# A scan kernel with an FFN in its shadow: FFN steps placed later in the phase, the normalisation's bias made on POOL, z statistics and x loads moved

## The reference

```
# layer 1, for each batch entry; channels = 512, states = 16
u     = silu(causal_conv4(in_proj(ctx)))                 # [512 channels, 512 steps]
dt_lo, Bm, Cm = x_proj(u)
delta = softplus(dt_proj(dt_lo) + bias)
state[t] = state[t-1] * exp(delta[t] * A) + delta[t]*u[t]*Bm[t]      # 16 states a channel
y     = (sum_n state_n * Cm_n + D*u) * silu(layernorm(x))
x     = x + tanh(g_xattn) * y
# layer 2
h     = layernorm(x)
sc    = h @ Wr                       # 32 experts
g     = softmax(sc) kept on the two highest, normalised (+1e-8)
out   = sum_s g_s * (h @ U_s) @ V_s;   gate = g @ sigmoid(attr @ Wa)
x     = x + tanh(g_ffn) * out * (0.9 + 0.2 * gate)
```

## Time and profile before

| what | value |
|---|---|
| median of 3 runs | 624.99 us (624.39 to 625.16) |
| the profiled execution | 624.96 us, its span 623.2 us |
| PE matmul busy | 538.7 us, 86% |
| DVE busy | 467.7 us, 75% |
| POOL busy | 437.2 us, 70% |
| ACT busy | 362.0 us, 58% |
| mean granted PE clock | 0.956 of full speed |

### The profile page before, as it was taken

The page is one execution under the profiler, slowest core; times in us unless marked ns, Lnnn a source line. Parts: engine busy times, 40 slices in busy tenths (PEclk is TensorE's granted clock), DMA queues, the critical chain, the costliest instruction groups (busy, mean ns, idle before and its releaser), DMA issues.

```text
span 623.2 us, 9369 instructions
## 1 busy us (share of the span) xinstructions
PE 538.7 (86%) x3410; PEld 415.3 (67%) x3410; DVE 467.7 (75%) x775; ACT 362.0 (58%) x574; POOL 437.2 (70%) x253
## 2 busy tenths in 40 slices
PE   6643979798868899999989999999988989986987
PEld 2142869777767687768777777677776868674443
DVE  3517989878848999788889999778779797944330
ACT  3343786857735667575756767566666676432311
POOL 0056999979996878669988788589978787741000
PEclk9765999999987899999999999999999999998899
DMA  3196000115220001035120000153000000000001
GB/s 83 54 359 232 2 0 2 35 51 192 101 69 1 1 1 52 1 116 210 35 85 2 18 1 19 62 197 102 17 2 18 1 19 1 17 18 1 18 17 50
DMA packets 17408, 35.19 MB, mean 56 GB/s; under 512 B 5441, under 2 KB 5953, under 8 KB 17362
## 3 DMA queue, kind: packets, MB, share of 16 engines
q1 hardware_dynamic: 17362, 34.60, 16.1%
HBM read 30.13 MB, written 4.46 MB: 56 GB/s over the span
## 4 chain that ended last, share of the span: by engine, by line
PE 38%; POOL 24%; DVE 15%; issue 10%; ACT 8%; DMA 3%; SPq 1%; DVEq 0%; POOLq 0%; ACTq 0%
POOL state L437 14%; PE p_s L575 10%; DVE state L1029 9%; PE p_y L593 7%; POOL dbu L428 6%; PE p_f L622 3%; ACT da L799 3%; PE p_tr L548 3%; PE p_v L631 3%; PE p_pr L521 3%; DMA xs<-in_x 2%; PE p_s L631 2%; POOL du L417 2%; POOL diag_b L407 1%; PE p_s L514 1%
## 5 line engine op out<-in xcount | busy, mean ns | idle before, releaser
L437 POOL TENSOR_TENSOR state<-state,c_bc 128x1024 f32<-128x1024 f32 x128 | 302.1, 2366 | 87.7 <-DVE state L1029 87.5
L1029 DVE TENSOR_TENSOR_SCAN state<-da,p_s 128x512 f32<-128x512 f32 x192 | 230.4, 1210 | 24.7 <-PE p_s L575 23.4
L575 PEld LDWEIGHTS p_s<-diag_b,du_t 128*128 128x128 f32 x1536 | 196.6, 198 | 26.7 <-issue 22.1
L575 PE MATMUL p_s<-diag_b,du_t 128*128 128x128 f32 x1536 | 209.8, 282 | 0.7 <-ACT du_t L775 0.7
L799 ACT ACTIVATE da<-delta,a_neg 128x512 f32<-128x512 f32 x192 | 136.2, 716 | 104.9 <-DVE state L1029 104.8
L593 PE MATMUL p_y<-ident,state 128*128 128x128 f32 x1024 | 144.2, 274 | 0.0
L593 PEld LDWEIGHTS p_y<-ident,state 128*128 128x128 f32 x1024 | 119.1, 142 | 10.1 <-issue 8.6
L1029 DVE TENSOR_TENSOR_SCAN state<-p_s,dbu 128x512 f32<-128x512 f32 x64 | 77.1, 1210 | 2.1 <-POOL dbu L428 2.1
L428 POOL TENSOR_TENSOR dbu<-du,b_bc 128x1024 f32<-128x1024 f32 x32 | 75.6, 2361 | 0.1
L799 ACT ACTIVATE p_s<-delta,a_neg 128x512 f32<-128x512 f32 x64 | 43.7, 688 | 28.9 <-DVE state L1029 28.7
L622 PE MATMUL p_f<-u_sb,h_t 128*128 128x512 f32 x96 | 47.7, 603 | 5.0 <-DVE gw L1118 5.0
(11 more groups left out here) (189 smaller groups left out, 621.6 us busy)
## 6 DMA issues: line engine op xcount, KB each, us to landing
c_bc<-bc_rows SPq DMA_DIRECT2D x32, 512.0 KB, 5.0
b_bc<-bc_rows SPq DMA_DIRECT2D x8, 512.0 KB, 4.5
xs<-in_x SPq DMA_DIRECT2D x16, 256.0 KB, 8.3
out<-ot SPq DMA_DIRECT2D x12, 256.0 KB, 2.0
cx<-in_ctx_t SPq DMA_DIRECT2D x4, 512.0 KB, 3.6
u_sb<-in_u_w SPq DMA_DIRECT2D x1, 1024.0 KB, 11.5
v_sb<-in_v_w SPq DMA_DIRECT2D x1, 1024.0 KB, 13.4
out<-state SPq DMA_DIRECT2D x4, 256.0 KB, 2.0
```

Of the source, the lines that this page charges most:

```text
L437: eng.tensor_tensor(pair, pair, c_bc[:, 2 * p:2 * p + 2, :], ALU.mult).then_inc(po_cs, 1)
L575: mm = eng.matmul(p_s[g % BANKS][:, t * P:(t + 1) * P], du_t[:, f % 2, t, :], diag_b[:, i, t, :], start=(t == 0), stop=(t == Q - 1))
L1029: eng.tensor_tensor_scan(slot(g), decayed, added, 0.0, ALU.mult, ALU.add).then_inc(ve_scan, 1)
```

## The change

Five edits.

1. Inside a phase, tile mid = f - 5: normed moves from the end of phase f - 1 (n = 15) to n = 1 of phase f, turn_h to n = 2, copy_h to n = 4, scores from n = 2 to n = 4, best_two to n = 4 and 5, exp_scores to n = 7, the gates from n = 4, 5, 6 to n = 6, 7, 8, with combine(f + 1) and gate_y(f - 1, 0) between their parts. times_u_weights moves from n = 8, 10, 12 to n = 10, 11, 12. turn_gated moves from n = 2 of the next phase to n = 15 of the same, copy_gated to n = 1 of the next. TURN and the head of the drain follow.
2. The bias of the normalisation is made by POOL, behind the power, and no longer by DVE (f_statistics part 3, L1067).
3. f_statistics parts 1 and 2 wait for POOL's work of four tiles earlier.
4. x of batch entry 0 is loaded ahead of C rows 5 to 7.
5. In phase 0 the z statistics move from n = 0 to 3 to n = 8 to 11, and scale_of_z(0) on POOL from after times_b(0, 5) to after times_c(0, 5).

```diff
@@ POOL
                 eng.tensor_tensor(fr[:, i, 0:1], fmv[:, i, 1:2], minus_half[:, 0:1], ALU.pow).then_inc(po_fs, 1)
+                eng.wait_ge(po_fs, 2 * T + 1)
+                eng.tensor_scalar(fr[:, i, 1:2], fmv[:, i, 0:1], fr[:, i, 0:1], -1.0, ALU.mult, ALU.mult).then_inc(po_fs, 1)
...
-                if k == 0:
+                if k == 0 and b:
                     scale_of_z(b)
...
+                if f == 0:
+                    scale_of_z(0)
                 times_c(f, 6)
@@ SP
-            for p in range(2, PAIRS):
+            for p in range(2, 5):
                 broadcast_c(0, p)
             for k in range(Q):
                 load_x(0, k)
+            for p in range(5, PAIRS):
+                broadcast_c(0, p)
@@ PE
                         if mid >= 0:
+                            turn_h(mid)
+                    if n == 4:
+                        if mid >= 0:
                             scores(mid)
-                        if tail >= 0:
-                            turn_gated(tail)
-                    if n == 4:
...
-                    if n == 8 and mid >= 0:
-                        times_u_weights(mid, [0, 1])
                     if n == 9 and f + 5 < F:
                         in_projection(f + 5)
                     if n == 10 and mid >= 0:
+                        times_u_weights(mid, [0, 1])
+                    if n == 11 and mid >= 0:
                         times_u_weights(mid, [2])
...
-                    if n == 15 and f >= Q:
-                        turn_h(f - Q)
+                    if n == 15 and mid >= 0:
+                        turn_gated(mid)
@@ DVE
-                    if f == 0 and n < Q:
-                        z_statistics(n)
+                    if f == 0 and 8 <= n < 8 + Q:
+                        z_statistics(n - 8)
...
-                    if n == 2 and mid >= 0:
+                    if n == 4 and mid >= 0:
                         best_two(mid, 0)
                         best_two(mid, 1)
-                    if n == 3 and mid >= 0:
+                    if n == 5 and mid >= 0:
                         best_two(mid, 2)
-                    if n == 4 and mid >= 0:
+                    if n == 6 and mid >= 0:
                         gates(mid, 0)
...
+                    if n == 7:
+                        if mid >= 0:
+                            gates(mid, 1)
+                        if f < LAST:
+                            combine(f + 1)
+                        if mid >= 0:
+                            gates(mid, 2)
+                    if n == 8:
+                        if mid >= 0:
+                            gates(mid, 3)
+                        if f:
+                            gate_y(f - 1, 0)
+                        if mid >= 0:
+                            gates(mid, 4)
+                            gates(mid, 5)
```

More of the change, by code:

```diff
@@ L77, in flamingo @@
             pass_through("sz", f - 1)
-        if f >= 6:
-            pass_through("hug", f - 6)
+        if f >= 5:
+            pass_through("h", f - 5)
         if f % Q == Q - 1 and f < LAST:
@@ L83, in flamingo @@
             pass_through("du", f + 1)
-        if f >= Q:
-            pass_through("h", f - Q)
-    for kind, i in [("sz", 15), ("hug", 10), ("h", 12), ("h", 13), ("hug", 11), ("h", 14), ("h", 15),
+        if f >= 5:
+            pass_through("hug", f - 5)
+    for kind, i in [("sz", 15), ("h", 11), ("h", 12), ("h", 13), ("hug", 11), ("h", 14), ("h", 15),
                     ("hug", 12), ("hug", 13), ("hug", 14), ("hug", 15)]:
@@ L227, in flamingo @@
         ve_fs = sem("dve_residual_statistics")
-        ve_nmr = sem("dve_residual_bias")
         ve_top = sem("dve_top")
@@ L703, in _ @@
             add_y(LAST, 9)
+            turn_h(11)
+            add_y(LAST, 10)
+            add_y(LAST, 11)
             scores(11)
-            add_y(LAST, 10)
-            turn_gated(10)
-            add_y(LAST, 11)
             add_y(LAST, 12)
@@ L826, in normed @@
             def normed(T):
-                eng.wait_ge(ve_nmr, T + 1)
+                eng.wait_ge(po_fs, 2 * T + 2)
                 if T and T < F - Q:
@@ L903, in _ @@
                         eng.activation(aw[:, :], y_rows[:, 0:S], ACT.Exp, scale=-1.0).then_inc(ac_k, 1)
-                    if n == 1 and mid >= 0:
-                        copy_h(mid)
+                    if n == 1:
+                        if mid >= 0:
+                            normed(mid)
+                        if tail >= 0:
+                            copy_gated(tail)
                     if n == 3:
@@ L910, in _ @@
                             place_residual(tail)
[L911 to L918, removed]
-                        softplus(f + 1, 0)
+                    if n == 4 and mid >= 0:
+                        copy_h(mid)
+                    if n == 5 and turning:
+                        copy_small(b + 1)
+                    if n == 7:
+                        if f < LAST:
+                            softplus(f + 1, 0)
+                        if mid >= 0:
+                            exp_scores(mid)
                     if n == 8:
@@ L939, in _ @@
                             copy_du(f + 1)
-                        if f >= Q:
-                            normed(f - Q)
                         if f + 5 < F:
                             tanh_v(f + 5)
+            normed(11)
+            copy_gated(10)
+            copy_sz(LAST)
             copy_h(11)
-            copy_sz(LAST)
             place_residual(10)
-            copy_gated(10)
             place_residual(11)
@@ L1058, in f_statistics @@
                     eng.wait_ge(ve_fs, FOPS * T + 1)
+                    if T >= Q:
+                        eng.wait_ge(po_fs, 2 * (T - Q) + 2)
                     eng.bn_aggr(fmv[:, i, :], fst[:, i, :]).then_inc(ve_fs, 1)
-                elif part == 2:
+                else:
                     eng.wait_ge(ve_fs, FOPS * T + 2)
+                    if T >= Q:
+                        eng.wait_ge(po_fs, 2 * (T - Q) + 2)
                     eng.tensor_scalar(fmv[:, i, 1:2], fmv[:, i, 1:2], EPS, None, ALU.add).then_inc(ve_fs, 1)
-                else:
-                    eng.wait_ge(po_fs, T + 1)
-                    if T >= Q:
-                        eng.wait_ge(ac_h, T - Q + 1)
-                    eng.tensor_scalar(fr[:, i, 1:2], fmv[:, i, 0:1], fr[:, i, 0:1], -1.0, ALU.mult, ALU.mult).then_inc(ve_nmr, 1)
             def best_two(T, part):
@@ L1226, in _ @@
                     gate_hu(11)
-            for T in range(F - Q, F):
-                f_statistics(T, 3)
             for T in (12, 13):
```

18 lines of the change are left out of this document (5 added, 13 removed).

## The result

| | before | after |
|---|---|---|
| median | 625.08 us (624.39 to 625.45, 4 runs) | 630.21 us (629.26 to 634.95, 4 runs) |
| profiled execution, span | 623.2 us | 628.1 us (629.87 in all) |
| PE matmul busy | 538.7 us | 539.5 us |
| DVE busy | 467.7 us | 457.3 us |
| POOL busy | 437.2 us | 440.6 us |

The account below looks back on a forecast made before the run. PE and DVE were taken as two bounds side by side. Terms: -6.0 - 5.6 + 3.4 + 1.8 + 3.4 + 7.6 + 0.5 + 4.0 + 1.9 - 8.8 = +2.2, so 627.2 us; 8 in 10: 613 to 637.

Parts of the forecast that it names:

- The cycle of a plain phase: Plain phases from 6 on: late gates make PE wait before times_u_weights, 8.7 + 24.5 = 33.2 us against 31.5, +1.7.
- Rival 4: Phases stay at 31.5 us because PE's idle time before times_u_weights does not appear: 609 us, chance 0.09.
- L1104's wait to the end of POOL's instruction: Gates after combine: L1104, issued 1.1 us into POOL's instruction, waits to its end; bounds 0.15 to 2.36 us.
- the early entry: Phase 5: L1104 gets in one POOL instruction earlier, giving -7.5 us instead of -5.2.
- main case: Phase 5: L1104 meets a POOL working without a gap until 213 and waits to about 202.6.
- Phases 4 and 5: DVE's 7.3 us wait at L1067 goes, with one fall of PE's clock counted: -5.6 us.
- Rival 2: L1104 gets in late in POOL's instruction, or another POOL order makes it cheap: 617 us, chance 0.10.
- The removed wait buys nothing here: Phases from 6 on: L1067's wait is gone, but DVE stands 2.9 us ahead of scan 6 waiting for make_dbu(6).
- PE's clock: Gaps before times_u_weights bring 1.2 GHz: +1.8 us in phases 6 to 10, +7.6 in 11 to 14, +1.9 in 15.
- rivals 1 and 3: 1: clock holds wholly or half, 614 or 620.5 us, 0.24; 3: falls in every phase 5 to 15, 638, 0.15.
- Head: Phase 0: z statistics no longer wait for x, first scan of phase 1 earlier: -6 us, bounds 0 and -8.
- Tail: Drain: normed(12) no longer waits for four tiles' statistics, times_u_weights(12) starts at 573.9 instead of 582.67: -8.8 us.

Follow-up runs that it names:

- the scalar form: Changed kernel with the first instruction of gates part 2 as tensor_scalar, its second number a scalar of each partition: 614.82 us, ratio 0.9849.
- edit 4 alone: Kernel before with only x of batch entry 0 loaded ahead of C rows 5 to 7, z statistics unmoved: 621.13 us, ratio 0.9941.

## Why the prediction was right, and where it was not

*The cycle of a plain phase.* Right: 33.2 us forecast, 33.16 measured; turning phases 37.6 and 37.23; f = 8 33.2 and 33.71; f = 9 32.2 and 32.03. L1110 about 1.3 us (1.29), 1.84 behind a turning phase, 0.15 beside scale_of_z; the idle time ahead of times_u_weights 2 and 4 us (1.70 and 4.07); cheap, the cycle is 32.0 (32.08). The two pieces, 8.7 and 24.5 us, came as 8.5 and 24.7. Rival 4 is out by the same numbers.

*L1104's wait to the end of POOL's instruction.* Right, also for a late start, which no row of before had shown. The trace agrees with the Trainium skill's rule (SBUF — State Buffer, SBUF: two separate sides), that whichever starts first holds the shared ports to its end. In phase 5 it came at 198.79, 0.26 us before POOL's instruction ended (199.05), and took 0.28. That isn't the early entry which the forecast had named as worth 2.3 us: counted from the combine in phase 4, it ended 33.9 us on, where the forecast's main case had it (202.6 less 168.67). Phases 4 and 5 came to -7.0 and not -5.6 because the fall of the clock that was counted in phase 5 didn't come: the gap there was 0.68 us, and from times_u_weights to scan 6 of phase 6 it was 25.0 us, 26.5 forecast. Rival 2 is out.

*"The removed wait buys nothing here".* Wrong as a statement of worth, though the sum did not need it. I compared the wait with DVE's idle time ahead of scan 6, one place, and not with the scans, ACT's decays and copies and the shared bank behind it. The new cycle was worked out directly for a DVE without the wait, so its number held. But edit 2 (with 3), which I priced at nothing outside phase 4 and the drain, is the best of the five, and the order, priced at 1.7 us a plain phase, costs 2.4 against a kernel that has edit 2 (30.76 to 33.16). In all it takes away those 13 us and some 8 more.

*PE's clock.* Right in place: no fall in phases 6 to 10 (1.8 forecast), one in each from 11 to 15, so rivals 1 and 3 are out. Off in size: 1.4 to 1.7 us for a fall instead of 1.9. From the combine in 14 on, two falls and an L1110 of 2.25 us stand in the +10.7, where 8.3 was forecast (0.5, 4.0 and two falls). I haven't taken that stretch apart. With the scalar form, which had a fall in phase 14 and none in 15, it (499.11 to 558.20) was 3.9 us longer than before.

*Head.* Wrong by 4.4 us, the largest miss of a term. Some 2.4 of it were there at the first scan of phase 1, half of that since the slow clock in phase 0 came that the -6 mostly left out. Then 2.0 more were lost: I followed ACT's queue behind z_part(0,0) to the decays, not to copy_du(1) and so not to PE. I had also put the gain down to the statistics and counted no gain for the x loads, where edit 4 alone gives 3.5 us and edit 5 adds nothing to it.

*Tail.* Mechanism right: normed(12) nearer, 14.9 us from gate_y(15,0) (570.98) to times_u_weights(12), 14.4 forecast; -8.2 of my -8.8. A fall of the clock behind it, at tile 13, took 1.7 back.

The errors stood on both sides (head +4.4, behind the combine in 14 +2.4 and tail +2.3; phases 6 to 14 -3.1, all of it clock, phases 4 and 5 -1.4, start -1.9), and the forecast was 2.7 us low against the profiled execution. The sizes of the main terms were right by their mechanism; that the sum came so near is in part luck, since misses of 9.1 us one way met 6.4 the other.

## What to carry to other kernels

A change of several edits hides its best one. Each edit wants its own price against the kernel it goes into (moving the bias was worth 13 us in one order of the steps and 17 to 19 in the other), and a wait that is taken out is priced by all that stands in the queue behind it, through the next engines, not by the idle time at one place. A step on which a saturated engine waits should not be put behind the work that is due last; and when the time ahead of such a step is long, the clock behind it can fall and is paid for too. Look first at instructions whose duration is ten times their work: changing the form of one, without changing what it computes, gave 3 to 15 us.

## What the runs showed of the hardware

- A DVE instruction on one number per partition with two tensors in SBUF took 1.29 or 1.84 us, to within 0.02 us of the end of POOL's tensor_tensor, when it began 1.1 or 0.5 us behind that one's start, and 0.15 us with POOL idle. The same sum with the second number as scalar took 0.20 us in all eleven phases.
- The idle time after which PE's clock falls has no sharp edge here: gaps of 2.98 us ahead of times_u_weights were followed by 1.98 us in one phase and by 3.64 and 3.27 in two others of the same run; 2.77 us left it at 2.4 GHz in one kernel and not in another; 1.70 to 2.25 us in phases 6 to 10 of after never brought it down. Shorter ones did elsewhere: 2.02 us in phase 15 was followed by 1.98 us in the changed kernel with the scalar form and by 3.64 with the bias back on DVE, and 1.94 us ahead of an input projection by 1.96 in before and by 2.72 with edit 4 alone.
- Eight matmuls that nobody reads, in each of four phases, made the kernel 4.5 us faster.
